# Four passes over the edges of a graph: where the gathers and the reloaded messages stand in their turns

## The reference

```python
h = jnp.maximum(_layernorm(x), 0.0)
for l in range(3):                              # L0: three layers
    edge_w = edge_attr_32 @ nn_w.T + nn_b       # [50000, 256]
    msg = jax.nn.relu(h[src] * edge_w)
    out = h @ root[l] + bias[l]
    for r in range(3):                          # three relations
        m = jnp.where((edge_type_3 == r)[:, None], msg, 0.0)
        mean = segment_sum(m, dst) / jnp.maximum(count(r, dst), 1.0)[:, None]
        out = out + mean @ W[l, r]
    h = out
x = x + h
h = jnp.maximum(_layernorm(x), 0.0)
gate = sigmoid(silu(edge_attr_64 @ W1 + b1) @ W2 + b2)   # L1: the gated pass
aggr = segment_sum(gate * h[src], dst)
x = x + silu(concat([h, aggr]) @ U1 + c1) @ U2 + c2
...                                             # L2 and L3: two attentions over the same edges
```

## Time and profile before

| what | us |
|---|---|
| median of 3 runs | 4755.39 (4747.29 to 4755.74) |
| profiled execution, span from first to last instruction (no other time is listed for it) | 4744.9 |
| PE busy | 3915.0 (83%) |
| PE weight loads busy | 3233.3 (68%) |
| DVE busy | 3382.7 (71%) |
| POOL busy | 3071.7 (65%) |
| ACT busy | 1791.0 (38%) |

### The profile page before, as it was taken

How to read it: one execution, slowest core, us unless ns; L and a number is a source line. 1 busy time by engine, 2 the same in 40 slices (tenths; PEclk the granted TensorE clock), 3 DMA queues, 4 the chain that set the end, 5 groups by cost and what they waited for, 6 DMA issues and landing times. The chain is left out here.

```text
span 4744.9 us, 105920 instructions
## 1 busy us (share of the span) xinstructions
PE 3915.0 (83%) x22300; PEld 3233.3 (68%) x22301; DVE 3382.7 (71%) x9318; ACT 1791.0 (38%) x5399; POOL 3071.7 (65%) x3178
## 2 busy tenths in 40 slices
PE   6799997889987889878899566779978778578886
PEld 3477775778776778767777556668866666366664
DVE  7799997667757778677787667874257778756666
ACT  0355553221123333333333100004257667367774
POOL 0266665777756777567775777766777773067774
PEclk9799998999998999989999777888978898778787
DMA  1233334856626445264452687861465444144445
GB/s 47 92 131 131 130 132 130 212 126 158 152 63 202 135 145 154 71 185 146 145 149 78 208 257 214 245 191 54 145 182 120 105 106 125 32 99 109 109 109 100
DMA packets 643665, 643.00 MB, mean 136 GB/s; under 512 B 314342, under 2 KB 549540, under 8 KB 643396
## 3 DMA queue, kind: packets, MB, share of 16 engines
q0 software_dynamic: 145840, 374.54, 27.8%
q1 hardware_dynamic: 443348, 213.36, 17.0%
q10 hardware_dynamic: 54336, 53.65, 3.3%
HBM read 470.09 MB, written 170.26 MB: 135 GB/s over the span
## 5 line engine op out<-in xcount | busy, mean ns | idle before, releaser
L1059 POOL DMA_INDIRECT G<-h_dram,idx x1572 | 1525.8, 971 | 556.8 <-issue 361.6
L1283 PEld LDWEIGHTS ps_a<-hotm,msg 128*128 128x128 f32 x4716 | 686.5, 193 | 196.2 <-DVE arena L1395 67.5
L1283 PE MATMUL ps_a<-hotm,msg 128*128 128x128 f32 x4716 | 730.0, 282 | 88.5 <-DVE arena L1395 87.8
L1271 PE MATMUL ps_e<-nnw,attT 128*128 128x256 f32 x2358 | 738.4, 396 | 76.8 <-DVE prodm L1388 42.4
L1395 DVE TENSOR_TENSOR arena<-ps_a,arena 128x256 f32 x1404 | 586.9, 418 | 218.8 <-issue 94.1
L735 POOL DMA_INDIRECT rec_dram<-rec,pos x392 | 376.7, 961 | 398.6 <-ACT rec L606 307.7
L1059 POOL DMA_INDIRECT G<-feat_dram,idx x420 | 402.4, 958 | 325.5 <-POOLq L241 197.9
L1317 ACT ACTIVATE msg<-prodm 128x256 f32<-128x256 f32 x786 | 327.5, 417 | 677.8 <-DVE prodm L1388 586.1
L749 POOL DMA_INDIRECT rec_dram<-rows,place x392 | 379.8, 969 | 222.1 <-issue 117.4
L1897 POOL DMA_INDIRECT arena<-rel_dram,idx x393 | 385.0, 980 | 128.6 <-issue 86.2
L1271 PEld LDWEIGHTS ps_e<-nnw,attT 128*128 128x128 f32 x2358 | 370.3, 195 | 118.4 <-DVE prodm L1388 56.4
(11 more groups left out here) (365 smaller groups left out, 7691.6 us busy)
## 6 DMA issues: line engine op xcount, KB each, us to landing
gate<-rec_dram SPq DMA_DIRECT2D x126, 384.0 KB
G<-msg_dram SPq DMA_DIRECT2D x300, 128.0 KB, 2.2
msg_dram<-msg ACTq DMA_DIRECT2D x270, 128.0 KB
rel_dram<-stage SPq DMA_DIRECT2D x25, 1040.0 KB
G<-h_dram,idx POOLq DMA_INDIRECT x1572
aT<-edge_attr SPq DMA_DIRECT2D x98, 128.0 KB
msg_dram<-arena ACTq DMA_DIRECT2D x90, 128.0 KB
attT<-attT_dram SPq DMA_DIRECT2D x74, 144.0 KB
```

The costliest lines, as they stand in the source:

```text
L1059: pool.indirect_dma_start(G[:, n % width, :], None, table, bass.IndirectOffsetOnAxis(ap=idx[:, which, n:n + 1], axis=0)).then_inc(sem(f"sw ...
L1271: t.matmul(ps_e[s % BANKS][:], attT[:, s // HU, s % HU, :], nnw[:], start=True, stop=True).then_inc(sem("ew"), 1)
L1283: last = t.matmul(ps_a[s % BANKS][:, h, :], of[:, h * P:(h + 1) * P], hot[:, s, :], start=True, stop=True)
```

## The change

`SEAM` goes from 11 to 1 and `BACK` from 5 to 3, so `FRONT` from 13 to 15. The first turn has 18 main units, each of the 25 others 15 main units and three extras. The totals stay: 18 + 25 x 15 = 393 main units, 75 extras, 468 units. Turns 0 to 4 store messages, as before, now 18 + 4 x 15 = 78 chunks. SP waits for the stores in two steps: for turn 0 before the extras of turn 1, and for all before those of turn `FIRST_KEPT` = 6. In layer 0 the columns of extras are loaded turn by turn, one turn ahead, and their rows are corrected turn by turn. At the start of layer 0 the columns of turns 1 and 2 come in four loads, where one load brought them. The diff, cut to its core:

```diff
-SEAM, BACK = 11, 5
+SEAM, BACK = 1, 3
 FRONT = U - BACK
 NU = SEAM * U + KD // BACK * U
 NC1 = SEAM * U + KD // BACK * FRONT
 KEPT = 5
+FIRST_KEPT = U // BACK
...
+        def stored_before(i, q, ring):
+            return U // ring + (i - 1) * len(range(q, FRONT, ring))
+
         def extra_messages(sp, G, ring=RING):
-            for q in range(ring):
-                sp.wait_ge(sem(f"msg_out{q}"), 16 * KEPT * U // ring)
+            def kept(i):
+                for q in range(ring):
+                    sp.wait_ge(sem(f"msg_out{q}"), 16 * stored_before(i, q, ring))
 
             def turn(i):
                 at = load_extras(sp, i - SEAM)
...
-            return turn
+            return kept, turn
...
                                 def extra_meta(t):
+                                    if not (isinstance(t, int) and t == 0):
+                                        sp.wait_ge(sem("extra_in"), t * BACK * 16)
                                     for j, at in enumerate(load_extras(sp, t)):
...
-                                    sp.wait_ge(sem("meta_in"), 16)
-                                    sp.dma_start(meta[:, U:3 * U, :], meta_rows[:, U:3 * U, :]).then_inc(sem("meta_in"), 16)
+                                    for t in range(1, 1 + AHEAD0):
+                                        for h in range(2):
+                                            columns_in(t, h)
                                     weights()
                                     extra_meta(0)
...
+                                    def turn(i, after, stored=0, ahead=AHEAD0):
                                         for h in range(2):
-                                            edge_rows(i, h, False, False)
-                                            columns_in(i + AHEAD0, h, False)
-                                            extra_meta(i * 2 - 1 + h)
...
+                                            edge_rows(i, h, after, True)
+                                            if ahead == AHEAD0:
+                                                columns_in(i + AHEAD0, h)
+                                        if ahead > 0:
+                                            extra_meta(i)
+                                        if stored:
+                                            kept(stored)
                                         extras(i)
+                                    turn(SEAM, False, 1)
+                                    with nc.sync.Fori(SEAM + 1, FIRST_KEPT) as i:
+                                        turn(i, True)
+                                    turn(FIRST_KEPT, True, KEPT)
+                                    with nc.sync.Fori(FIRST_KEPT + 1, TURNS1 - AHEAD0) as i:
+                                        turn(i, True)
...
-                                for c0, c1, c3, c4 in walk(nc.scalar, TURNS1, 0, 1, 3, 4, seams=(KEPT, SEAM), late=True):
+                                for c0, c1, c3, c4 in walk(nc.scalar, TURNS1, 0, 1, 3, 4, seams=(SEAM, KEPT), late=True):
...
-                                    if c4 and c4.phase == 0:
+                                    if c4 and c4.phase <= 1 and not c4.extra:
...
-                                        if l == 0 and isinstance(n, int) and n == SEAM * U:
-                                            dve.wait_ge(sem("extra_in"), 16 * KD)
-                                            rows = late_meta[:, :, FRONT:U, 0]
-                                            v.scalar_tensor_tensor(rows, iota[:, 1:KD + 1].rearrange("p (t j) -> p t j", j=BACK), -float(P), rows,
+                                        if l == 0 and s == HU and c0.late:
+                                            dve.wait_ge(sem("extra_in"), i * BACK * 16)
+                                            rows = late_meta[:, ds(i - SEAM), FRONT:U, 0].rearrange("p t s -> p (t s)")
+                                            v.scalar_tensor_tensor(rows, iota[:, ds((i - SEAM) * BACK + 1, BACK)], -float(P), rows,
                                                                    ALU.mult, ALU.add).then_inc(sem("extra_rows"), 1)
-                                            dve.wait_ge(sem("extra_rows"), 1)
+                                            dve.wait_ge(sem("extra_rows"), i)
```

More of the change, by code:

```diff
@@ L124, in at @@
         if s >= lag:
-            return None if last else Unit(i * width + (s - lag), i, s - lag, phase, late and phase == len(seams))
-        return None if first else Unit(i * width + (s - lag), i - 1, s - lag + width, before, late and before == len(seams))
+            return None if last else Unit(i * width + (s - lag), i, s - lag, phase, late and phase > 0)
+        return None if first else Unit(i * width + (s - lag), i - 1, s - lag + width, before, late and before > 0)
     for s in range(width):
@@ L131, in walk @@
     for phase, end in enumerate((*seams, turns - static)):
-        with eng.Fori(begin, end) as i:
-            for s in range(width):
-                yield [at(i, s, lag, False, False, phase, phase) for lag in lags]
+        if begin < end:
+            with eng.Fori(begin, end) as i:
+                for s in range(width):
+                    yield [at(i, s, lag, False, False, phase, phase) for lag in lags]
         begin = end
@@ L1138, in weights, with columns_in @@
                                     sp.dma_start(bias[:], L0_gnn_bias[l:l + 1, :].to_broadcast([P, D])).then_inc(sem("w_in"), 16)
[L1140 to L1152, removed]
+                                def columns_in(turn, half):
+                                    sp.wait_ge(sem("meta_in"), (turn * 2 - 1 + half) * 16)
+                                    lo, hi = ((0, HU), (HU, FRONT))[half]
+                                    sp.dma_start(late_meta[:, ds(turn - SEAM), lo:hi, :].rearrange("p t s w -> p (t s) w"),
+                                                 rec_d[ds((turn * FRONT + SEAM * BACK + lo) * P, (hi - lo) * P), WMETA:WMETA + NMETA].rearrange(
+                                                     "(j p) w -> p j w", p=P)).then_inc(sem("meta_in"), 16)
                                 def edge_rows(i, h, after, late):
@@ L1193, in _ @@
[L1193 to L1206, removed]
-                                        for h in range(2):
-                                            edge_rows(i, h, True, True)
-                                            columns_in(i + AHEAD0, h, True)
-                                        extras(i)
@@ L1211, in _ @@
-                                    with nc.sync.Fori(TURNS1 - AHEAD0, TURNS1) as i:
-                                        for h in range(2):
-                                            edge_rows(i, h, True, True)
-                                        extras(i)
+                                            edge_rows(i, h, after, True)
[3 more added lines that the diff above has]
+                                            extra_meta(i)
@@ L1215, in _ @@
+                                    for ahead in reversed(range(AHEAD0)):
+                                        turn(TURNS1 - 1 - ahead, True, ahead=ahead)
                                 else:
@@ L1358, in _ @@
+                                        for k in turns_in if not (isinstance(i, int) and i + AHEAD0 >= TURNS1) else ():
+                                            dve.wait_ge(sem("meta_in"), k * 32 + 16)
+                                            v.tensor_copy(idx[:, 0, ds(k * U, FRONT)],
+                                                          late_meta[:, ds(k - SEAM), 0:FRONT, 1].rearrange("p t s -> p (t s)")).then_inc(sem("columns"), 1)
                                     if c0 and c0[2] % HU == 0:
@@ L1525, in gates, with turn @@
                                         "(j p) w -> p j w", p=P)).then_inc(sem(f"gate_in{q}"), 16)
-                            with nc.sync.Fori(0, SEAM) as i:
-                                gates(i, False, False)
-                            extras = extra_messages(sp, G, RING1)
-                            gates(SEAM, False, True)
-                            extras(SEAM)
-                            with nc.sync.Fori(SEAM + 1, TURNS1) as i:
-                                gates(i, True, True)
-                                extras(i)
+                            gates(0, False, False)
+                            kept, extras = extra_messages(sp, G, RING1)
+                            def turn(i, after, stored=0):
+                                gates(i, after, True)
+                                if stored:
+                                    kept(stored)
+                                extras(i)
+                            turn(SEAM, False, 1)
+                            with nc.sync.Fori(SEAM + 1, FIRST_KEPT) as i:
+                                turn(i, True)
+                            turn(FIRST_KEPT, True, KEPT)
+                            with nc.sync.Fori(FIRST_KEPT + 1, TURNS1) as i:
+                                turn(i, True)
```

62 lines of the change are left out of this document (30 added, 32 removed).

## The result

The changed kernel takes 4706.35 us (median of four runs, 4701.79 to 4716.86), the kernel before 4755.57 (four runs, 4747.29 to 4758.13). The ratio is 0.9908 with a 95% interval of 0.9896 to 0.992: 49 us or 0.9% faster. The profiled execution of after took 4708.06 us around a span of 4706.3, 38.6 us less than the span of the earlier trace rows.

The account below looks back on a forecast made before the run. Gathers bound the early turns, compute engines the last ones. Gains of 13 (layer 0), 16.8 (layer 1), 18.1 (layer 2) and 1.3 (gated pass) sum to 49.2 us: 4755.4 - 49.2 = 4706 us, 8-in-10 range 4688 to 4738.

Parts of the forecast that it names:

- Gathers as the floor of layers 1 and 2: Layers 1 and 2: gathers at 1.25 us each, 490.0 us first to last, set the pace; gains 16.8 and 18.1 us.
- The tail: End of layers 1 and 2: 2.8 us for the last gather's landing and 6.8 to the end, 9.6 us.
- The hold-ups: Layers 1 and 2: gathers held up by the shorter lead and the store turns, 2 us charged to each.
- a sign of being wrong: Layers 1 and 2: GpSimd waiting for products in most turns would show the forecast wrong.
- Layer 0, the term that was mis-sized: Layer 0: engines at 19.7 us a turn and gathers at 19.9 are level; gain 13 us, ends 0 and 23.
- the start: Start of layer 0: four column loads in place of one land about when VectorE wants them; 2 us charged.
- Gated pass: Gated pass: 393 gathers at 1.28 us stay as they are, only the tail shortens; gain 1.3 us.
- the bad end: Gated pass: store turns limited by DMA at 311 GB/s lose 1.0 us in each of four turns, 4 us.
- The slower rival: Layers 0 to 2: register reads before adds stay as long in all turns as in store turns; 4827 us, 5%.
- my sign of being wrong: VectorE's idle time before the adds at 2 us a turn throughout would show the forecast wrong.
- SyncE's queue: Wait for turn 0's stores before turn 1's extras: a cover of 11 us, so nothing charged.

Follow-up runs that it names:

- fewer_gathers: The changed kernel with two of the 15 gathers of every turn from the second on left out in layers 1 and 2; 4681.87 us.
- more_dve_late: The changed kernel with two additions of 128 x 256 more a turn on VectorE in layers 1 and 2; 4729.62 us.
- no_stores: The changed kernel without message stores, and the waits for them, in layers 1 and 2 and the gated pass; 4699.94 us.
- reads_3: The changed kernel with VectorE's bucket numbers read in six batches of three a turn, not two of nine, in layers 0 to 2; 4697.62 us.
- numbers_reads_3: The changed kernel with register reads in batches of three and layer 0's row of numbers from PSUM together; 4677.61 us.
- psum_numbers: The changed kernel with layer 0's one-hots reading the row of numbers from PSUM in place of SBUF; 4711.63 us.
- no_stores_layer0: The changed kernel without the message stores of turns 1 to 4 in layer 0 alone; 4708.07 us.

## Why the prediction was right

- *Gathers as the floor of layers 1 and 2*: right, and shown by fewer_gathers, more_dve_late and no_stores. The terms were too large by 6.8 and 2.2 us. The tail is 11.6 and 11.7 us instead of 9.6, mostly the landing of 4.25 instead of 2.8. The hold-ups (what the gathers take beyond 490.0 us) are 6.7 us in layer 1 and 2.3 in layer 2, instead of 2. They lie in the store turns and just behind them (1515 to 1567 us in layer 1). For these turns the prediction read 18.75 us from eight one-hots in 75 us; by their adds they took 20.0 us each in layer 1 before and 20.8 after. The hold-ups come from the stores by way of the reads: no_stores removes them, and so does reads_3, which leaves the stores and shortens the reads. ScalarE's waits for stored messages aren't the way: in numbers_reads_3 they are 4.3 us in layer 2, and its gathers still take 490.2. From 1567 us on every gather started on pace, so GpSimd waiting for products in most turns, a sign of being wrong, didn't come.
- *Layer 0, the term that was mis-sized*: 13 us predicted, 3.9 measured. By the engines alone my sum gave 12.3, less 2 for the start; I went above that towards the gathers' side, and the engines set it (psum_numbers). A late turn takes 19.96 us, not 19.7; turns 1 to 4 lose 13.4 us, not 8.8; the last turn, 15.9 us, gives 3.8 back. The prediction counted the reads' idle time there, but not the clock that falls behind it. From the first gather, the first turn ended 1.9 us later than before, as much as I charged, but the four column loads are not the cause (GpSimd waited 0.3 us for them): a read left 1.82 us of idle time before an add there against 1.57 before, and from 816 to 836 us the granted clock was 0.91 against 1.00.
- *Gated pass*: 1.3 predicted, 6.5 measured. Its tail is 12.1 us instead of 14.6, and its gathers take 498.6 us instead of 502.6, since fewer of them run long (65 with 8.0 us above the common time, 100 with 12.0 before). Why fewer do was not tried; in the eleven profiles of changed kernels, after with them, the pass takes 509.3 to 511.9 us. The 4 us of the bad end didn't come: 331 GB/s at a full DMA share, where the row's ceiling was 311. The 358 GB/s of the Trainium skill (HBM Reference, Specifications) was not reached in this stretch either.
- *The slower rival* (reads as long in all turns as in those with stores) asked for 1.3 us more of idle time a turn. Late in layer 0, "issue" before the adds did rise by that much, from 3.4 / 8 = 0.4 us a turn to 1.8, but not because the reads grew. They are as long as before (before from 1190 to 1340 us, then after from 1000 to 1340):

```profile
L187 DVEq TENSOR_LOAD <-bmap x16: 846/2210/2527, 1195.9 to 1336.7; - x16
...
L187 DVEq TENSOR_LOAD <-bmap x34: 850/2209/2511, 1003.3 to 1332.9; - x34
```

  The read takes the place of a wait for TensorE that is no longer there. The adds of before, in the stretch of the earlier trace rows:

```profile
L1395 DVE TENSOR_TENSOR arena<-ps_a,arena 128x256 f32 x145 | 60.3, 416 | 22.6 <-PE ps_a L1283 17.5 <-issue 3.4 <-DVE arena L1395 1.7
```

  All idle time before the adds is 39.0 / 17 = 2.3 us a turn in after and 22.6 / 8 = 2.8 before. So my sign of being wrong, 2 us a turn throughout, was no sign: the kernel before shows it as well.
- *SyncE's queue* cost nothing, as said; no engine's waits, in any of the four passes, name a reloaded message.

## What to carry to other kernels

When two streams of work share a loop and their shares differ between its halves, add up each stream over the whole pass and even them out turn by turn: here the slower stream, the gathers, ran hardly faster than before, but half as much was left to do behind its last one. A pause that an engine makes for a batch of register reads is to be cut into pieces that its queued work covers, and to be priced with the slower clock that TensorE may show after it. Where two bounds lie side by side, a change to the hinder one alone shows nothing: psum_numbers gained 0 us alone and 13 behind reads_3.

## What the runs showed of the hardware

- TensorE's granted clock fell to half (1.2 GHz) after pauses of 1.57 (before 820.7 in after), 1.93, 2.88 (before 868.4 in after) and 3.37 us. It stayed full after pauses of 1.72 us, after three of 1.92 to 1.94 us late in layer 1 of no_stores_layer0, and after one of 2.72 us (before 2105.9 in after).
- Reads of three, nine and eighteen registers on VectorE's queue mostly take 0.75, 2.07 and 4.08 us in quiet turns, 0.22 us a further value. In layer 0's store turns the median of nine is 3.04 us, and 2.24 with the stores of turns 1 to 4 left out.
- Gathers of layer 0 run long, up to 2.1 us instead of 0.95, under one-hots that VectorE makes from two SBUF inputs, and not one does when one input is in PSUM. The Trainium skill (SBUF — State Buffer, Who interferes with whom) names a port pair that VectorE and GpSimd share, and psum_numbers bears it out.
